# A graph attention layer on one core: a ring of 16 for the gathered rows, loads and stores on other queues in the first stages, a shorter last stage

## The chip, the cores and the metric

The kernel runs on one core of a Trainium2 chip. The metric is the device time of one execution in microseconds (us). The core has a tensor engine (PE, with its weight load shown apart as PEld), a vector engine (DVE), a scalar engine (ACT), a general engine (POOL, GpSimd) and a sync engine (SP) that here only issues transfers. ACT, SP and POOL each have a DMA queue, and an engine that issues a transfer does nothing else in that time.

## The reference

A graph has N = 12500 nodes with 96 features and E = 412500 edges sorted by destination. Keys, queries and values come from the nodes, a factor from each edge; each edge gives 8 heads a weight, and the destination sums weighted values.

```python
Q_h, K_h, V_h = [(x @ W + b).reshape(N, 8, 12) for W, b in ((Wq, bq), (Wk, bk), (Wv, bv))]
E = (edge_attr @ We + be).reshape(-1, 8, 12)
score = K_h[src] * Q_h[dst] / sqrt(12) * E
score = exp(clip(score.sum(-1, keepdims=True), -5.0, 5.0))
wV = segment_sum(V_h[src] * score, dst); Z = segment_sum(score, dst)
out = layernorm(x + wV / (Z + 1e-06))
```

## The kernel before, in words

Every engine runs its own program, written out by hand, and waits on semaphores; no scheduler moves anything.

**First stage** (25 batches of 500 nodes). Per batch: a load of x (`load_x`, two transfers: 112 rows and 13 rows) into a ring of 4 (`x_in`), four transposes on PE, a copy to `xT` (which shares its memory with `accT`) by ACT, four matmuls with the key and value weights, copies to `kv_out` (a ring of 4) by ACT and DVE, and two transfers to `kv_dram`, the table of keys and values. SP issues the loads and the stores alike, in one program (`node_batch`). The matmuls need a row of ones under `xT`, which POOL writes. POOL also loads the edge lists (`dst_nat`, `src_nat`), converts them and stores the destinations in 16 bits. From batch 9 on PE and DVE put in, between batches, 7 blocks of destinations and 7 of sources (`turn`, `destinations`, `sources`: tables `rel` and `src_tab`). When the last is done, DVE makes the least destination of each chunk (`ranges`), POOL stores it and loads it back as the tables `base_tab`, `extra_tab` and `base_all`.

**Query stage** (25 batches). PE makes the queries; ACT and DVE split them into three bf16 parts in `q_out`, a ring of 4 batches (semaphores `q_first`, `q_second`, `q_parts_ready`); SP stores them to `q_dram`. Ahead of the first such store SP issues six transfers of edge features (`load_edges`) and two of destinations. In the middle DVE runs `tables`: it subtracts `base_all` from `rel`.

**Main loop** (806 chunks of 512 edges). POOL gathers the rows of the sources, four indirect transfers (`indirect_dma_start`) per chunk of 128 rows of 768 bytes, into the ring `kv` of RING = 8 chunks; for chunk s it waits until the messages of chunk s-8 are made (`msg_ready`), and, every fourth chunk, until ACT has copied the next four chunks of indices (`copy_sources`, `src_copied`; ACT's step s copies those of chunk s + IDX_AHEAD). ACT makes a one-hot matrix of the destinations, PE turns it into the queries and projects the edge features, DVE multiplies (`kqe`), sums per head, makes the messages, and adds the sums of each chunk into `accT`. SP loads the queries of 8 chunks ahead, ACT the edge features of 15 chunks ahead. At step -1 DVE and ACT each set half of `accT` to zero.

**Last stage** (25 batches). PE transposes `accT`, DVE adds 1e-6 to Z, takes its reciprocal and multiplies, POOL adds x, DVE takes the statistics, ACT the square root and the scaling, SP stores.

Of the kernel before, what the change touches and what calls it, by code (L numbers as in the profile page):

```python
# [5 lines left out]
ALU = mybir.AluOpType  # L6
# [7 lines left out]
P = 128  # L14
HEADS = 8
G = 4
# [14 lines left out]
RING = 8  # L31
HALF = RING // 2
# [5 lines left out]
IDX_AHEAD = 8  # L38
# [3 lines left out]
NOWHERE = -1.0e6  # L42
# [7 lines left out]

def run_steps(engine, step, chunks, lag, round_values=None, lead=0, unroll=RING, ahead=0):

    rounds = (chunks - 1 - ahead) // unroll
    for s in range(-lead, unroll):
        step(s, s % unroll, None)
    with engine.Fori(1, rounds) as i:
# [7 lines left out]
def run_batches(engine, step, batches, lag, shift=0, unroll=4):  # L64

    rounds = (batches - 1 - shift) // unroll
# [9 lines left out]
def gnn_kernel(nc, x, src, dst, edge_attr, Wq, bq, Wk, bk, We, be, Wv, bv, out):  # L79
# [26 lines left out]
    with ExitStack() as ctx:  # L106
# [3 lines left out]
        def sem(name):  # L110
# [14 lines left out]
        kv_mem = sb("kv_mem", [P, RING * G * 2 * D])  # L125
# [5 lines left out]
        src_nat = ea_mem[0:NQ, 0:NJ * CHUNK]  # L131
        dst16 = ea_mem[0:NQ, NJ * CHUNK:NJ * CHUNK * 3 // 2].bitcast(I16)
        q_out = ea_mem[:, NJ * CHUNK * 3 // 2:NJ * CHUNK * 3 // 2 + 2 * BATCH * PARTS * D].bitcast(BF16).rearrange(
            "p (u j k d) -> p u j k d", j=BATCH, k=PARTS, d=D)
        msg_mem = sb("msg_mem", [P, MSG_RING * G * DZ])
        msg = msg_mem[:, :].rearrange("p (c g f) -> p c g f", g=G, f=DZ)
        q_rest = msg_mem[:, 0:2 * BATCH * D].rearrange("p (u j d) -> p u j d", j=BATCH, d=D)
        zero = sb("zero", [P, 1])
# [4 lines left out]
        spare = sb("spare", [P, NJ * CHUNK])  # L143
        dst_nat = spare[0:NQ, 0:NJ * CHUNK]
# [9 lines left out]
        extra_tab = sb("extra_tab", [1, C], I32)  # L154
        most = sb("most", [1, 1], I32)
        base_all = sb("base_all", [P, C], I32)
        minus_id = sb("minus_id", [SEL, C])
        rel = sb("rel", [P, C * G])
        src_tab = sb("src_tab", [P, C * G])
# [16 lines left out]
        x_res = spare[:, 0:4 * BATCH * D].rearrange("p (u j d) -> p u j d", j=BATCH, d=D)  # L176
# [4 lines left out]
        eps = sb("eps", [P, 1])  # L181
        std = sb("std", [P, 2, BATCH])
# [16 lines left out]
        ones_ready = sem("ones_ready")  # L199
        zero_set = sem("zero_set")  # L200
# [46 lines left out]
        kv_in = [sem(f"kv_in{i}") for i in range(RING)]  # L247
# [43 lines left out]
        eps_set = sem("eps_set")  # L291
        rooted = sem("rooted")
# [19 lines left out]
        def landed(engine, sems, c, u, per_load):  # L312

            if isinstance(c, int):
                engine.wait_ge(sems[u], per_load * (c // RING + 1))
# [822 lines left out]
```

## Time and profile before

| | |
|---|---|
| time, median of 3 runs | 4268.54 us (4266.72 to 4269.54) |
| the profiled execution | 4274.5 us, of which the span of its trace is 4272.3 us |
| PE busy | 3085.4 us, 72% of the span |
| DVE busy | 2724.9 us, 64% |
| ACT busy | 1402.3 us, 33% |
| POOL busy | 3164.7 us, 74% |
| bytes moved | 612.49 MB, 143 GB/s over the span |

Busy time leaves out the issue of transfers on ACT and SP; POOL's indirect transfers are counted as busy time of POOL. "Granted clock" is that of the tensor engine, as a share of its full speed of 2.4 GHz.

### The profile page before, as it was taken

To read this page: it belongs to the slowest core of one execution; us is meant where nothing else is said; L and a number is where in the kernel's file an instruction comes from. 1 tells how busy PE (TensorE), PEld (TensorE's weight loads), DVE (VectorE), ACT (ScalarE), POOL (GpSimd) and SP (SyncE) were. 2 spreads that over 40 slices of the span, in tenths; PEclk is the share of its full clock that TensorE was granted. 3 is DMA by queue.
4 is the path that set the end of the run, shared out by engine and by line. 5 is a ranking of instruction groups with operands and counts; after the bars stand their busy time and mean duration, and the time that the engine had idled before them with its cause. 6 is when DMAs were issued, how large, how long until landed. Compare 5 with 4: busy or idle time off the path is not lost.

```text
span 4272.3 us, 62447 instructions
## 1 busy us (share of the span) xinstructions
PE 3085.4 (72%) x16776; PEld 2975.1 (70%) x16777; DVE 2724.9 (64%) x6880; ACT 1402.3 (33%) x3655; POOL 3164.7 (74%) x3356
## 2 busy tenths in 40 slices
PE   6687777777777777777777777777777777777775
PEld 5687766777767677767777767677677766767774
DVE  3676666666666666666666666666666666666667
ACT  2433333333333333333333333333333333333334
POOL 4577777777777777777777777777777777777775
PEclk8555555555555555555555555555555555555555
DMA  7776666666666666666666666666666666666653
GB/s 196 185 154 140 145 140 141 142 143 142 140 144 140 140 143 143 142 139 145 142 138 146 142 140 144 140 142 142 143 142 138 146 140 141 143 142 142 140 129 108
DMA packets 1533277, 612.49 MB, mean 143 GB/s; under 512 B 1392691, under 2 KB 1453694, under 8 KB 1533249
## 3 DMA queue, kind: packets, MB, share of 16 engines
q0 software_dynamic: 156864, 321.70, 30.1%
q10 hardware_dynamic: 1244934, 238.82, 29.4%
q1 hardware_dynamic: 131451, 51.67, 4.9%
q8 instruction: 9, 0.15, 0.0%
q14 instruction: 19, 0.16, 0.0%
HBM read 589.46 MB, written 22.46 MB: 143 GB/s over the span
## 4 chain that ended last, share of the span: by engine, by line
POOL 52%; issue 20%; DMA 12%; DVE 9%; POOLq 1%; DVEq 1%; ACT 0%; ACTq 0%
POOL kv_mem L564 52%; DMA kv_mem<-kv_table,src_idx 12%; DVE kqe L991 2%; DVE kqe L988 2%; DVE msg_mem L1003 2%; DVE oh L1000 1%; DVE raw_score L995 0%; DVE y_stats L1097 0%; DVEq L323 0%; DVE eaT L1011 0%; POOLq L48 0%; ACTq L368 0%; POOLq L562 0%; DVE z_inv L1086 0%; DVE mean_var L1110 0%
## 5 line engine op out<-in xcount | busy, mean ns | idle before, releaser
L564 POOL DMA_INDIRECT kv_mem<-kv_table,src_idx x3224 | 3085.3, 957 | 1012.6 <-issue 928.5
L680 PE MATMUL bank<-w_e,eaT 97*128 97x96 f32 x6448 | 1627.4, 434 | 1076.2 <-DVE eaT L1011 1073.8
L680 PEld LDWEIGHTS bank<-w_e,eaT 97*128 97x128 f32 x6448 | 1440.2, 328 | 1165.7 <-DVE eaT L1011 1159.1
L690 PE MATMUL bank<-oh,msg_mem 128*104 128x32 f32 x6448 | 1258.1, 359 | 7.8 <-DVE msg_mem L1003 7.8
L690 PEld LDWEIGHTS bank<-oh,msg_mem 128*104 128x104 f32 x6448 | 1211.1, 293 | 8.3 <-DVE msg_mem L1003 8.3
L988 DVE TENSOR_TENSOR kqe<-kv_mem,bank 128x384 f32<-128x384 f32 x806 | 445.7, 553 | 1046.0 <-DMA kv_mem<-kv_table,src_idx 1041.9
L797 ACT ACTIVATE msg_mem<-score 128x32 f32<-128x32 f32 x806 | 184.7, 229 | 2711.9 <-DVE score L1017 2464.1
L803 ACT ACTIVATE away<-dst_b,minus_id 96x512 bf16<-96x512 int16 x806 | 568.6, 705 | 0.0
L1011 DVE STREAM_TRANSPOSE eaT<-ea_mem 96x512 f32<-96x512 f32 x806 | 564.8, 701 | 0.0
L806 ACT ACTIVATE ohT<-away 96x512 bf16<-96x512 bf16 x806 | 507.3, 629 | 25.5
L991 DVE TENSOR_TENSOR kqe<-kqe,bank 128x384 f32<-128x384 f32 x806 | 446.1, 553 | 27.8
L995 DVE TENSOR_REDUCE raw_score<-kqe 128x32 f32<-128x384 f32 x806 | 445.5, 553 | 27.8
L1003 DVE TENSOR_TENSOR msg_mem<-kv_mem,bank 128x384 f32<-128x384 f32 x806 | 438.3, 544 | 0.0
L684 PE MATMUL bank<-q_win,ohT 96*128 96x96 bf16 x3224 | 425.2, 283 | 9.5 <-DMA q_win<-q_table 9.5
L684 PEld LDWEIGHTS bank<-q_win,ohT 96*128 96x128 bf16 x3224 | 414.4, 161 | 17.5 <-DMA q_win<-q_table 10.0
L985 DVE TENSOR_TENSOR accT<-bank,accT 104x32 f32 x806 | 154.7, 192 | 331.2 <-DVE score L1017 162.8
L1000 DVE TENSOR_TENSOR oh<-bank,rel 128x128 f32<-128x128 f32 x806 | 226.4, 281 | 6.4 <-ACT bank L799 6.3
L1017 DVE TENSOR_SCALAR score<-raw_score 128x32 f32<-128x32 f32 x806 | 150.2, 186 | 0.0
L799 ACT ACTIVATE bank<-score 128x32 f32<-128x32 f32 x806 | 147.3, 183 | 0.1
L651 PE MATMUL bank<-w_kvq,accT 97*125 97x96 f32 x200 | 36.7, 372 | 23.5 <-DVE msg_mem L949 22.7
L651 PEld LDWEIGHTS bank<-w_kvq,accT 97*125 97x125 f32 x200 | 35.8, 285 | 24.4 <-DVE msg_mem L949 23.4
L587 POOL TENSOR_TENSOR kv_mem<-kv_mem,spare 125x384 f32<-125x384 f32 x25 | 25.0, 1001 | 34.5 <-DVE kv_mem L1091 34.4
(93 smaller groups left out, 516.5 us busy)
## 6 DMA issues: line engine op xcount, KB each, us to landing
ea_mem<-in_edge_attr_dram ACTq DMA_DIRECT2D x591, 256.0 KB
dst_b<-dst_by_chunk ACTq DMA_DIRECT2D x199, 408.0 KB
kv_mem<-kv_table,src_idx POOLq DMA_INDIRECT x3224
q_win<-q_table SPq DMA_DIRECT2D x806, 19.9 KB
kv_table<-kv_mem SPq DMA_DIRECT2D x25, 336.0 KB
q_table<-ea_mem SPq DMA_DIRECT2D x25, 252.0 KB
kv_mem<-in_x_dram SPq DMA_DIRECT2D x25, 168.0 KB
spare<-in_x_dram SPq DMA_DIRECT2D x25, 168.0 KB
```

The lines of the kernel that those rows point to most:

```text
L564: pool.indirect_dma_start(kv[:, slot, g, :], None, kv_dram[:, :], bass.IndirectOffsetOnAxis(ap=src_idx[:, u, g:g + 1], axis=0)).then_inc(k ...
L680: nc.tensor.matmul(e_ps[v][:, g * D:(g + 1) * D], eaT[:, v, g * P:(g + 1) * P], w_e[:, :], start=True, stop=True)
L684: last = nc.tensor.matmul(q_ps[v][:, g * D:(g + 1) * D], ohT[:, u, g * P:(g + 1) * P], q_win[0:SEL, u, :], start=(g == 0), stop=(g == G - ...
L690: last = nc.tensor.matmul(sum_ps[v], msg[:, w, g, :], oh[:, w % DEPTH, g, :], start=(g == 0), stop=(g == G - 1), skip_group_check=True)
L803: nc.scalar.activation(away[:, u % 2, :], dst_b[0:SEL, w, :], ACT.Abs, bias=minus_id[:, bass.ds(t, 1)]).then_inc(away_done, 1)
L806: nc.scalar.activation(ohT[:, w, :], away[:, u % 2, :], ACT.Relu, bias=1.0, scale=-1.0).then_inc(ohT_built, 1)
L988: nc.vector.tensor_tensor(kqe[:, :, :], kv[:, ua, :, 0:D], q_ps[v][:, 0:G * D].rearrange("p (g d) -> p g d", g=G), ALU.mult).then_inc(kq_d ...
L991: nc.vector.tensor_tensor(kqe[:, :, :], kqe[:, :, :], e_ps[v].rearrange("p (g d) -> p g d", g=G), ALU.mult).then_inc(kqe_done, 1)
L995: nc.vector.tensor_reduce(raw_score[:, :], kqe[:, :, :].rearrange("p g (h d) -> p (g h) d", d=HD), AX_X, ALU.add).then_inc(heads_summed, 1)
L1000: nc.vector.tensor_tensor(oh[:, um % DEPTH, :, :], column_ps[um % DEPTH].unsqueeze(1).to_broadcast((P, G, WIN)), rel[:, bass.ds(m * G, G)] ...
L1003: nc.vector.tensor_tensor(msg[:, um % MSG_RING, :, 0:D].rearrange("p g (h d) -> p g h d", d=HD), kv[:, um, :, D:2 * D].rearrange("p g (h d ...
L1011: nc.vector.transpose(eaT[0:D, w % DEPTH, :], ea[:, w, :]).then_inc(ea_turned, 1)
```

## The change

The change has four parts. (1) The rows' ring `kv` has KV_RING = 16 chunks; POOL may run `room` chunks ahead, 16 for the first chunks and one fewer every 6 chunks down to 8; the copies of the indices run 12 chunks ahead, and 16 chunks of indices are copied before the main loop. To make space `rel` and `src_tab` are of 16 bits, and the edge lists and `q_out` lie elsewhere. (2) In the first stage ACT's queue issues the loads of x, SP's only the stores; DVE writes the ones under `xT`, batch by batch; the store of the pad rows and the edge loads come later on SP. ACT's queue stores the queries. (3) POOL loads the three tables back after its first chunk of gathers. (4) 1e-6 is laid into `accT`'s rows of Z at the start (so DVE's half is set in two instructions), the addition in the last stage falls away, and ACT loads the table of the square root once ahead of the last stage.

```diff
-IDX_AHEAD = 8
+IDX_AHEAD = 12
+KV_RING = 16
-        kv_mem = sb("kv_mem", [P, RING * G * 2 * D])
+        kv_mem = sb("kv_mem", [P, KV_RING * G * 2 * D])
-        rel = sb("rel", [P, C * G])
-        src_tab = sb("src_tab", [P, C * G])
+        rel = sb("rel", [P, C * G], I16)
+        src_tab = sb("src_tab", [P, C * G], I16)
...
         @block.sync
-            def node_batch(b, u):
-                if not isinstance(b, int) or 4 <= b < BATCHES:
-                    sp.wait_ge(x_turned, b - 3)
-                    load_x(sp, b, u)
-                if not isinstance(b, int) or b >= 3:
...
+            def store_rows(b, u):
+                sp.wait_ge(kv_evac_act, b + 1)
+                sp.wait_ge(kv_evac_dve, b + 1)
+                for lo, hi in NODE_PARTS:
+                    sp.dma_start(kv_t[lo:hi, bass.ds(b * BATCH, BATCH), :], kv_out[lo:hi, u, :, :]).then_inc(kv_stored[u], 16)
...
-            sp.wait_ge(src_turned, NJ)
             sp.wait_ge(dst16_stored, 32)
-            for g in range(2):
-                load_edges(sp, g * EA_GROUP, g)
             for h in range(2):
                 load_destinations(sp, h * HALF, h)
-            def store_queries(b, u):
...
+            sp.wait_ge(src_made, NJ + 1)
+            load_edges(sp, 0, 0)
+            sp.wait_ge(q_parts_ready, BATCHES // 2)
+            load_edges(sp, EA_GROUP, 1)
...
         @block.gpsimd
-            nc.gpsimd.memset(xT[D:DA, 4 * BATCH * NP:N], 1.0).then_inc(ones_ready, 1)
...
             def step(s, u, _):
-                slot = u % RING
-                at_least(pool, msg_ready, s - RING + 1)
+                slot = u % KV_RING
+                if isinstance(s, int) and s == 1:
+                    load_tables()
+                room = max(KV_RING // 2, KV_RING - max(0, s - KV_RING) // 6) if isinstance(s, int) else KV_RING // 2
+                at_least(pool, msg_ready, s - room + 1)
...
         @block.scalar
             def node_batch(b, u):
...
+                if not isinstance(b, int) or b + 4 < BATCHES:
+                    load_x(act, b + 4, u)
...
-            for s in range(0, IDX_AHEAD, IDX_GROUP):
+            for s in range(0, IDX_RING, IDX_GROUP):
                 copy_sources(s, s)
             def query_batch(b, u):
...
+                if not isinstance(b, int) or b >= 2:
+                    v = (u - 2) % 4
+                    act.wait_ge(q_parts_ready, b - 1)
+                    for lo, hi in NODE_PARTS:
+                        act.dma_start(q_t[lo:hi, bass.ds((b - 2) * BATCH, BATCH), :, :], q_out[lo:hi, v, :, :, :]).then_inc(q_stored[v], 16)
...
+            nc.scalar.activation(table_warm[:, :], eps[:, :], ACT.Sqrt)
...
         @block.vector
             for b in range(1, BATCHES + 1):
+                if b + 3 < BATCHES:
+                    nc.vector.memset(xT[D:DA, (b + 3) * BATCH * NP:(b + 4) * BATCH * NP], 1.0).then_inc(x_ones_set, 1)
...
-                    nc.vector.memset(accT[:, 0:N // 2], 0.0).then_inc(acc_zeroed, 1)
+                    nc.vector.memset(accT[0:D, 0:N // 2], 0.0)
+                    nc.vector.memset(accT[D:P, 0:N // 2], 1e-6).then_inc(acc_zeroed, 1)
...
-                    nc.vector.tensor_scalar(zi, sums[:, :, D:DZ], 1e-6, None, ALU.add).then_inc(z_step, 1)
+                    nc.vector.reciprocal(zi, sums[:, :, D:DZ]).then_inc(z_step, 1)
                 if first:
-                    dve.wait_ge(z_step, 2 * b + 1)
-                    nc.vector.reciprocal(zi, zi).then_inc(z_step, 1)
```

SP's queue between the first and the query stage, before: the last stores of keys and values, the edge features, the destinations, then the first stores of queries (the names are destination <- source and the shape).

```order
L404 DMA kv_table<-kv_mem 112x768 [waits kv_evac_dve,kv_evac_act]
L404 DMA kv_table<-kv_mem 13x768
L368 DMA ea_mem<-in_edge_attr_dram 32x64x32 [waits dst16_stored,src_turned]
L368 DMA ea_mem<-in_edge_attr_dram 32x64x32 x5
L384 DMA dst_b<-dst_by_chunk 102x2048 x2
L437 DMA q_table<-ea_mem 112x1152 [waits q_parts_ready]
L437 DMA q_table<-ea_mem 13x1152
```

The same place now: three edge transfers follow the destinations, three more wait for the middle of the query stage, and no store of queries is on this queue.

```order
L405 DMA kv_table<-kv_mem 112x768 [waits kv_evac_dve,kv_evac_act]
L405 DMA kv_table<-kv_mem 13x768
L413 DMA q_table<-pad_rows 44x288 [waits pad_zeroed]
L390 DMA dst_b<-dst_by_chunk 102x2048 [waits dst16_stored]
L390 DMA dst_b<-dst_by_chunk 102x2048
L374 DMA ea_mem<-in_edge_attr_dram 32x64x32 [waits src_made]
L374 DMA ea_mem<-in_edge_attr_dram 32x64x32 x2
L374 DMA ea_mem<-in_edge_attr_dram 32x64x32 [waits q_parts_ready]
```

POOL from the loads of the tables to chunk 9, before.

```order
L552 DMA base_tab<-chunk_base 1x13x62 [waits range_stored]
L553 DMA extra_tab<-chunk_extra_windows 1x13x62
L554 DMA base_all<-chunk_base 128x806
L564 DMA kv_mem<-kv_table,src_idx 128x192 [waits kv_stored3,src_copied,kv_stored2,kv_stored0,kv_stored1]
L564 DMA kv_mem<-kv_table,src_idx 128x192 x15
L564 DMA kv_mem<-kv_table,src_idx 128x192 [waits src_copied]
L564 DMA kv_mem<-kv_table,src_idx 128x192 x15
L564 DMA kv_mem<-kv_table,src_idx 128x192 [waits msg_ready,src_copied]
L564 DMA kv_mem<-kv_table,src_idx 128x192 x3
```

The same now, up to chunk 16: the first wait for a message stands behind 64 gathers instead of 32, and the tables' loads behind the first four.

```order
L565 DMA kv_mem<-kv_table,src_idx 128x192 [waits dst16_stored,kv_stored3,src_copied,kv_stored2,kv_stored0,kv_stored1]
L565 DMA kv_mem<-kv_table,src_idx 128x192 x3
L546 DMA base_tab<-chunk_base 1x13x62 [waits range_stored]
L547 DMA id_mem<-chunk_extra_windows 1x13x62
L548 DMA base_all<-chunk_base 128x806
L565 DMA kv_mem<-kv_table,src_idx 128x192 x12
L565 DMA kv_mem<-kv_table,src_idx 128x192 [waits src_copied]
...
L565 DMA kv_mem<-kv_table,src_idx 128x192 [waits msg_ready,src_copied]
L565 DMA kv_mem<-kv_table,src_idx 128x192 x3
```

ACT in the first stage now, one batch in the middle: the two loads of x stand between its two copies (before, only the copies were there).

```order
L753 ISA [waits x_turned]
L753 COPY accT<-bank 96x500
L395 ISA
L395 DMA kv_mem<-in_x_dram 112x384
L395 ISA
L395 DMA kv_mem<-in_x_dram 13x384
L760 ISA [waits kv_stored1]
L761 COPY kv_mem<-bank 125x384 [waits kv_done]
```

## Rows read from the trace of the kernel before

**Rows 1.** Page, part 5, main loop: line, engine, count, busy, mean ns, idle before.

```profile
L564 POOL DMA_INDIRECT kv_mem<-kv_table,src_idx x3224 | 3085.3, 957 | 1012.6 <-issue 928.5
...
L1000 DVE TENSOR_TENSOR oh<-bank,rel 128x128 f32<-128x128 f32 x806 | 226.4, 281 | 6.4 <-ACT bank L799 6.3
```

**Rows 2.** Timeline of POOL: start, duration, line, [idle before <- what ended it].

```profile
99.40 1.06 POOL L564 DMA_INDIRECT kv_mem<-kv_table,src_idx  x1 [2.03 <-issue]
...
135.58 4.34 POOL L564 DMA_INDIRECT kv_mem<-kv_table,src_idx  x1 [0.30 <-issue]
...
172.68 0.95 POOL L564 DMA_INDIRECT kv_mem<-kv_table,src_idx  x1 [28.98 <-DVE msg_mem L1003]
...
4194.34 0.95 POOL L564 DMA_INDIRECT kv_mem<-kv_table,src_idx  x1 [0.30 <-issue]
```

**Rows 3.** Waits in 0 to 100 us: total, times, longest.

```profile
PE bank L610 <- DMA kv_mem<-in_x_dram: 24.9, 14, 12.7
```

**Rows 4.** Timeline of SP's queue in the first stage.

```profile
20.57 0.31 SPq L411 DMA_DIRECT2D q_table<-pad_rows  x1
...
83.55 0.86 SPq L404 DMA_DIRECT2D kv_table<-kv_mem  x2
84.62 0.87 SPq L389 DMA_DIRECT2D kv_mem<-in_x_dram  x2
```

**Rows 5.** Windows: length, busy of each engine (count), granted clock, DMA share, GB/s.

```profile
0.00:50.00 50.00, 23.42 (x108) 21.01 (x110) 7.60 (x18) 10.84 (x20) 41.67 (x50) 0.72 0.68 189
50.00:100.00 50.00, 43.27 (x303) 40.14 (x302) 30.15 (x61) 20.00 (x41) 4.25 (x8) 0.97 0.70 200
```

**Rows 6.** Timeline of DVE and ACT in one batch of the first stage.

```profile
82.16 0.64 DVE L891 COPY src_tab<-bank 128x460 f32<-128x460 f32 x1 [0.43 <-PE bank L632]
...
82.59 0.57 ACT L753 COPY accT<-bank 96x500 f32<-96x500 f32 x1 [0.99 <-PE bank L610]
82.71 0.55 DVE L876 COPY kv_mem<-bank 125x384 f32<-125x384 f32 x1
83.18 0.68 DVE L888 TENSOR_REDUCE lohi<-spare 115x1 f32<-115x512 f32 x1
83.30 0.48 ACT L759 COPY kv_mem<-bank 125x384 f32<-125x384 f32 x1
...
93.51 0.56 DVE L876 COPY kv_mem<-bank 125x384 f32<-125x384 f32 x1 [0.74 <-PE bank L625]
```

**Rows 7.** Timeline of POOL: loads of the tables.

```profile
95.79 0.50 POOL L552 DMA_DIRECT2D base_tab<-chunk_base  x1 [4.06 <-DMA chunk_extra_windows<-lohi_end_i]
...
96.77 0.60 POOL L554 DMA_DIRECT2D base_all<-chunk_base  x1
```

**Rows 8.** Timeline of the query stage, ACT, DVE and SP's queue.

```profile
108.19 50.43 SPq L437 DMA_DIRECT2D q_table<-ea_mem  x50
118.95 0.48 ACT L780 CAST ea_mem<-bank 125x384 bf16<-125x384 f32 x1 [19.82 <-DMA q_table<-ea_mem]
119.33 0.52 ACT L784 CAST ea_mem<-msg_mem 125x384 bf16<-125x384 f32 x1
...
135.59 3.50 DVE L921 TENSOR_TENSOR rel<-rel,base_all 128x3224 f32<-128x3224 f32 x1
...
156.10 1.22 DVE L953 TENSOR_TENSOR ea_mem<-msg_mem,ea_mem 125x384 bf16<-125x384 f32 x2
```

**Rows 9.** Timeline of DVE and ACT as the main loop starts.

```profile
160.76 5.27 DVE L1014 MEMSET accT<- 128x6250 f32 x1 [1.26 <-issue]
...
166.95 0.56 DVE L988 TENSOR_TENSOR kqe<-kv_mem,bank 128x384 f32<-128x384 f32 x1 [0.93 <-PE bank L684]
...
182.50 0.19 ACT L768 CAST src_idx<-src_tab 128x16 int32<-128x16 f32 x1
```

**Rows 10.** Timeline of DVE in the last stage, one batch apart.

```profile
4218.23 0.16 DVE L1083 TENSOR_SCALAR z_inv<-bank 125x32 f32<-125x32 f32 x1
...
4220.51 0.16 DVE L1083 TENSOR_SCALAR z_inv<-bank 125x32 f32<-125x32 f32 x1
```

More of the change, by code:

```diff
@@ L41 @@
 BATCH = 4
[L42 removed]
+NOWHERE = -20000
 def at_least(engine, sem, value):
@@ L48, in at_least, with run_steps @@
         engine.wait_ge(sem, value)
-def run_steps(engine, step, chunks, lag, round_values=None, lead=0, unroll=RING, ahead=0):
+def run_steps(engine, step, chunks, lag, round_values=None, lead=0, unroll=RING, ahead=0, first=1):
     rounds = (chunks - 1 - ahead) // unroll
-    for s in range(-lead, unroll):
+    for s in range(-lead, first * unroll):
         step(s, s % unroll, None)
-    with engine.Fori(1, rounds) as i:
+    with engine.Fori(first, rounds) as i:
         values = [None] * unroll if round_values is None else round_values(i)
@@ L61, in run_steps, with run_batches @@
         step(s, s % unroll, None)
-def run_batches(engine, step, batches, lag, shift=0, unroll=4):
-    rounds = (batches - 1 - shift) // unroll
+def run_batches(engine, step, batches, lag, shift=0, unroll=4, ahead=0):
+    rounds = (batches - 1 - shift - ahead) // unroll
     for b in range(unroll + shift):
@@ L246, in gnn_kernel @@
         slots_taken = sem("slots_taken")
-        kv_in = [sem(f"kv_in{i}") for i in range(RING)]
+        kv_in = [sem(f"kv_in{i}") for i in range(KV_RING)]
         pe_step = sem("pe_step")
@@ L566, in step @@
                                             ).then_inc(kv_in[slot], 16)
-            run_steps(pool, step, C, 0, unroll=IDX_RING)
+            run_steps(pool, step, C, 0, unroll=IDX_RING, first=4)
             def gather(c):
@@ L616, in node_batch @@
                         pe.wait_ge(w_kvq_in, 16 * 6)
-                    if isinstance(b, int) and b == 4:
-                        pe.wait_ge(ones_ready, 2)
                     m = b - 1
+                    at_least(pe, x_ones_set, m - 3)
                     pe.wait_ge(x_copied, b)
@@ L807, in step @@
                     if isinstance(s, int) and s == -1:
-                        nc.scalar.copy(accT[:, N // 2:N], zero[:, 0:1].to_broadcast((P, N - N // 2))).then_inc(acc_zeroed, 1)
+                        nc.scalar.copy(accT[:, N // 2:N], acc_first[:, 0:1].to_broadcast((P, N - N // 2))).then_inc(acc_zeroed, 1)
                     if w % HALF == HALF - 1 and (not isinstance(t, int) or t + HALF + 1 < C):
                         load_destinations(act, t + HALF + 1, w // HALF)
-                if u % IDX_GROUP == 0 and (not isinstance(s, int) or s >= 0):
+                if u % IDX_GROUP == 0 and (not isinstance(s, int) or s > 0):
                     copy_sources(s + IDX_AHEAD, (u + IDX_AHEAD) % IDX_RING)
@@ L854, in _ @@
             nc.vector.memset(eps[:, :], EPS_LN).then_inc(eps_set, 1)
+            nc.vector.memset(acc_first[0:D, :], 0.0).then_inc(acc_first_set, 1)
+            nc.vector.memset(acc_first[D:P, :], 1e-6).then_inc(acc_first_set, 1)
             nc.vector.memset(zero[:, :], 0.0).then_inc(zero_set, 1)
```

71 lines of the change are left out of this document (35 added, 36 removed).

## The prediction

> **What bounds the kernel now.** I read the page first, for the main loop. POOL's indirect transfers take 3085.3 us and are followed by idle time put down to "issue" [rows 1]: 957 ns of work and about 0.30 us of gap, 1.26 us per gather and 5.04 us per chunk. Nothing else is as slow, and nearly all that POOL waits for is its own issue. So I went to POOL's timeline for the only times when it does not run at that pace [rows 2]. It starts at 99.40, makes 32 gathers (the ring of 8 chunks is full), stands still for 28.98 us until DVE has made the first messages, starts again at 172.68 and runs to 4195.29 (4194.34 + 0.95). From 172.68 that is 798 chunks in 4022.6 us, 5.041 us each, without one stop. The time of the kernel is therefore: the start of POOL's first gather (99.4), 806 chunks at 5.041 (4063.0), a stop of 28.7 beyond the usual gap, 4.2 us of disturbed gathers, and 77.0 us from the last gather to the end of the span (4272.3). The edit touches the first, third and last of these; the rate stays.
>
> **First stage (POOL's first gather).** That gather waits for the stores of keys and values; the last copy to `kv_out` ends at 94.07 [rows 6] and the gather follows 5.3 us later. What holds the stage is the loads of x: PE waits 24.9 us for them in 14 pieces, the longest of 12.7 us [rows 3], because SP stands until 20.57 at the pad store, behind POOL's memset, with everything queued behind it [rows 4]. Later SP needs 0.86 for a pair of stores and 0.87 for a pair of loads, beside their waits; the pair-to-pair pace there is about 2.2 us at best. Now ACT issues the loads right after its copy of x, four batches ahead, and SP has half its work.
>
> What binds next? DVE's rows for a batch with a turned block are 0.64 + 0.55 + 0.68 [rows 6]; the new memset of 500 columns is estimated from the one of 6250 columns, 5.27 us or, with the unexplained 1.26 us ahead of it, 6.53 [rows 9], so 0.42 to 0.52. Together 2.4 us. ACT has 0.57 + 0.48 and a pair of issues, 0.87 by SP's row: 1.9 us. The transfers: 189 GB/s over 50 us and 200 GB/s over the next 44 [rows 5] are 18.3 MB, and 200 GB/s took a share of 0.70, so 286 GB/s and 64 us if the DMA engines were never idle. At nine tenths of that it is 71 us, against 25 x 2.4 = 60 us plus a start of some 8 us by DVE. The two bounds lie close together; I take the last copy at 72.7, so the first gather at 78.0: **-21.4 us**. Bounds: DMA engines always full, copy at 64.5, gather at 70 (-29); only something like the 12.7 us gap is saved and the rest paces on (-10).
>
> **Tables.** POOL's three loads (95.79 to 97.37, [rows 7]) move behind the first chunk's gathers. They no longer wait 4.06 us for the ranges to be stored, since five microseconds of gathers lie between; but what lay in the shadow of the stores of keys and values now stands between gathers: **+1.6 us**, at most 3.6 if the 2.03 us idle ahead of the first gather [rows 2] comes twice.
>
> **The stop of POOL.** It vanishes if POOL is never out of room or of indices. It needs its first message and the indices of chunks 16 to 19 when it has made 64 gathers: 16 x 5.04 + 1.6 + 4.2 = 86.4 us after its start, at 164.5. Those indices are copied in ACT's step 4, which before came at 182.50, 15.6 us after the first `kqe` at 166.95 [rows 9]. When is the first `kqe` now? I let the query stage start 1.7 us after the last copy, at 74.4. Before, ACT waited 19.82 us in it because SP's edge transfers stood ahead of the stores of queries [rows 8]; these are now on ACT. ACT's batch is 0.48 + 0.52 [rows 8] + a pair of issues of 0.87 = 1.87 us, 47 us for 25. Half the edge transfers still compete; SP's 50 stores took 50.43 us with gathers beside them, or 2.0 per batch. I take 53 us: the last part at 127.5. From there to `kqe` it took 9.6 us (157.32 to 166.95); the second memset on DVE adds up to 6.5: 143.6. Then the indices come at 159.2, 5 us ahead of need. The later groups are looser: POOL needs 20.2 us for four chunks, while DVE's busy time is 3.4 us per chunk (2724.9 / 806) and PE's 3.8 (3085.4 / 806), so both catch up. So the stop goes wholly: **-28.7 us**. The bound on the other side: each microsecond that the query stage takes beyond 58 us comes back one for one.
>
> **What the earlier gathers meet.** Of POOL's first 32 gathers one took 4.34 us instead of 0.96, beside DVE's L921 of 3.50 us [rows 2, 8], and the others lost 0.9 us together (143.70 - 99.40 = 44.3 us, against 40.0 at 1.26 each), beside some 16 of the L953. Before, that was hidden by the stop in part; in my sum it stays in full, and the other nine L953 add **+0.5 us**. L921 reads two tensors from SBUF. The Trainium skill's page "SBUF — State Buffer", section "Who interferes with whom", says that such an instruction contends with a GpSimd instruction that reads SBUF, but also that a probe did not see `tensor_tensor` delay the writing of descriptors. By the second half the disturbance would be nothing and the sum some 4 us lower, 4212; the row of 4.34 us speaks against that.
>
> **Last stage.** One batch takes DVE 2.28 us (4218.23 to 4220.51, [rows 10]), it never waits there, and 0.16 of it is the addition that falls away, with a little of a semaphore: 0.18 x 25, **-4.5 us** (bounds 0, if ACT or POOL takes over the pace, and 5). The early load of the square root's table costs ACT nothing, it stands idle then. The rows of Z starting at 1e-6 cost nothing but the second memset, already counted.
>
> **Sum.** -21.4 - 28.7 + 1.6 + 0.5 - 4.5 = -52.5 us. The profiled execution, 4274.5, becomes 4222.0; it stands 6.0 above the median of the runs shown, 4268.5, so the forecast for a median is **4216 us**.
>
> **Rivals.**
> A. *The first stage doesn't speed up much*, because transfers are slower when more of them are in flight: gather at 89, so -10 instead of -21: 4227. For it: the share is 0.70 already [rows 5]. Against: PE's waits are of the loads' lateness, not their length.
> B. *The new wait for indices or messages.* If the query stage takes 65 us instead of 53, for ACT now issues inside it and waits for `q_stored` with a ring of 4, POOL stops for about 7 us at chunk 16: 4223; at 75 us, 4233. For it: by the same start of 1.7 us the old stage took 157.3 - 95.8 = 61.5 us, though 19.8 of them were the block by edges.
> C. *DVE's memsets hold POOL.* POOL was standing while L1014 ran, so no row shows it. If they held it as L921 did, two of 6.5 us would add 13: 4229. Against: L1000, with one input from SBUF, leaves the gather's mean at 957 ns [rows 1]. The page named above agrees with this: an instruction with at most one SBUF input outside the two-port modes does not contend; by it the 13 us are nothing.
> D. *Slower than before: a gather gets longer in the main loop.* The only instruction of the loop whose operand changes type is L1000, which reads `rel`, now in 16 bits; it takes 281 ns per chunk [rows 1]. If it held POOL for all of that, 806 x 0.281 = 226 us would be lost: 4442. It decides from 52.5 us / 806 = 65 ns per chunk, 16 ns per gather. Against: it has one input from PSUM before and after, and POOL's gap does not feel it now.
> E. *Both gains are larger*: the gather starts at 70, and the disturbances shrink: 4205.
>
> **How the numbers follow.** Forecast with its small terms (4208 to 4224) 0.56; A 0.14; B 0.12; C 0.06; D 0.04; E 0.08. The range from 4201 to 4238 leaves out D, the worst of B and the extremes of A with C, and less than 2 in 10. A difference of 0.2% (8.5 us) is about what can be told from no change. All but D, and A, B and C together (0.02), are beyond it: faster 0.94, same 0.02, slower 0.04.
>
> **What would show it.** In the changed kernel's trace: the first gather at 74 to 82 and not near 89; PE's wait for x under 8 us; no idle of POOL above 3 us before the last gather, in particular none at chunk 16, 20 or 24; a spacing of gathers of 1.26 us; one gather of about 4.3 us beside the subtraction; none stretched beside the memsets; the last gather at about 4148; a batch of the last stage in 2.1 us. The prediction is wrong if POOL stops at chunk 16, if its first gather comes after 88, or if the mean of a gather is not 957 ns.

## The result, and the profile after

The changed kernel takes 4206.73 us (median of 4 runs, 4204.96 to 4207.62); the kernel before beside it took 4268.74 us. The ratio is 0.9855, with a 95% interval from 0.9838 to 0.9872: 62 us faster, 10 us more than forecast, and inside the forecast range of 4201 to 4238. The profiled execution of the changed kernel took 4206.3 us, its span 4204.4 us.

POOL's timeline is the one to read first, as before. Start, duration, line, [idle before <- what ended it].

```profile
70.71 1.05 POOL L565 DMA_INDIRECT kv_mem<-kv_table,src_idx  x1 [5.81 <-DMA kv_table<-kv_mem]
...
74.62 0.96 POOL L565 DMA_INDIRECT kv_mem<-kv_table,src_idx  x1 [0.30 <-issue]
75.58 0.56 POOL L546 DMA_DIRECT2D base_tab<-chunk_base  x1
...
76.67 0.59 POOL L548 DMA_DIRECT2D base_all<-chunk_base  x1
...
101.14 4.50 POOL L565 DMA_INDIRECT kv_mem<-kv_table,src_idx  x1 [0.30 <-issue]
...
136.76 0.95 POOL L565 DMA_INDIRECT kv_mem<-kv_table,src_idx  x1 [0.30 <-issue]
...
158.20 0.95 POOL L565 DMA_INDIRECT kv_mem<-kv_table,src_idx  x1 [0.39 <-issue]
...
4130.10 0.95 POOL L565 DMA_INDIRECT kv_mem<-kv_table,src_idx  x1 [0.31 <-issue]
```

The first gather starts at 70.71 instead of 99.40 [rows 2], the three table loads stand behind the fourth gather, the 65th gather (chunk 16) starts at 158.20 with 0.39 us of idle time ahead of it, and nothing stops POOL until its last gather ends at 4131.05. The stop of 28.98 us has no counterpart.

The first stage, in the waits of 0 to 100 us (total, times, longest), the windows (busy time of PE, PEld, DVE, ACT and POOL, granted clock, DMA share, GB/s) and SP's queue:

```profile
PE bank L611 <- DMA kv_mem<-in_x_dram: 6.0, 6, 4.0
```

```profile
0.00:50.00 50.00, 40.68 (x249) 37.61 (x251) 31.49 (x66) 19.21 (x37) 32.75 (x49) 0.97 0.91 293
...
20.00:25.00 5.00, 4.30 (x28) 3.71 (x27) 2.46 (x6) 2.38 (x6) 4.78 (x5) 1.00 1.03 389
...
50.00:60.00 10.00, 9.97 (x75) 9.57 (x73) 9.23 (x18) 5.25 (x10) 0.00 (x0) 1.00 0.68 206
```

```profile
9.74 57.12 SPq L405 DMA_DIRECT2D kv_table<-kv_mem  x50
66.91 1.26 SPq L413 DMA_DIRECT2D q_table<-pad_rows  x1
```

PE's waits for x are 6.0 us instead of 24.9 [rows 3], the stores begin at 9.74, and 293 GB/s moved in the first 50 us instead of 189 [rows 5], at times 389. Near the end of the stage the transfers are not what it waits for: from 50 to 60 us their share is 0.68, and PE is busy for 9.97 of the 10 us. The clock granted to PE in the first 50 us is 0.97 instead of 0.72 [rows 5]; before, PE did nothing from 15 to 20 us, and the clock was 0.50, its lower level, from 20 to 30.

The start of the main loop, on DVE and ACT:

```profile
129.67 5.27 DVE L1028 MEMSET accT<- 96x6250 f32 x1 [1.26 <-issue]
136.28 5.27 DVE L1029 MEMSET accT<- 32x6250 f32 x1 [1.34 <-issue]
141.58 0.55 DVE L1002 TENSOR_TENSOR kqe<-kv_mem,bank 128x384 f32<-128x384 f32 x1
...
145.93 0.55 DVE L1017 TENSOR_TENSOR msg_mem<-kv_mem,bank 128x384 f32<-128x384 f32 x1
...
157.22 0.19 ACT L770 CAST src_idx<-src_tab 128x16 int32<-128x16 int16 x1
```

The page, part 5, and DVE's timeline in the last stage, one batch apart:

```profile
L565 POOL DMA_INDIRECT kv_mem<-kv_table,src_idx x3224 | 3076.2, 954 | 988.2 <-issue 937.6
```

```profile
4188.17 0.33 DVE L1098 RECIPROCAL z_inv<-bank 125x32 f32<-125x32 f32 x1
...
4190.22 0.33 DVE L1098 RECIPROCAL z_inv<-bank 125x32 f32<-125x32 f32 x1
```

A batch takes 2.05 us, against 2.28 [rows 10]. A gather is 954 ns instead of 957 [rows 1]; from the 65th gather to the last their distance is 1.2573 us, in the profile of before 1.2602. So the 67.9 us between the two spans are:

| term | us |
|---|---|
| first gather, 99.40 to 70.71 | -28.7 |
| the stop | -28.7 |
| distance of gathers, 3223 x 0.0029 | -9.4 |
| table loads between gathers (distance of the fourth and fifth is 2.94) | +1.7 |
| stretched gathers: 5.3 us in all, 4.5 before | +0.9 |
| from the last gather's end to the end of the span, 77.0 to 73.35 | -3.7 |

Two of these were not in the forecast at this size: the first, and the third, which was not in it at all.

### The profile page after: what moved, and what is told of

It reads as the page before. It is cut to its first block, busy times and chain, and to the rows that moved or that the text cites. A ratio compares the mean times of both kernels' runs of the same rounds, so it can differ in the third digit from the quotient of the medians.

```text
span 4204.4 us, 62289 instructions
## 1 busy us (share of the span) xinstructions
PE 3076.6 (73%) x16776; PEld 2970.3 (71%) x16777; DVE 2718.5 (65%) x6879; ACT 1402.2 (33%) x3656; POOL 3146.7 (75%) x3355
## 4 chain that ended last, share of the span: by engine, by line
POOL 54%; issue 21%; DMA 12%; DVE 9%; DVEq 1%; PE 1%; POOLq 1%; SPq 1%; ACT 0%; ACTq 0%
POOL kv_mem L565 54%; DMA kv_mem<-kv_table,src_idx 10%; DVE kqe L1005 2%; DVE kqe L1002 2%; DVE msg_mem L1017 2%; DMA q_table<-msg_mem 1%; DVEq L329 1%; DVE oh L1014 1%; DVE eaT L1025 1%; PE bank L625 1%; DVE raw_score L1009 0%; DVE y_stats L1109 0%; SPq L374 0%; POOLq L49 0%; DMA q_win<-q_table 0%
## 5 line engine op out<-in xcount | busy, mean ns | idle before, releaser
L810 ACT ACTIVATE away<-dst_b,id_mem 96x512 bf16<-96x512 int16 x806 | 568.7, 706 | 1.7 <-issue 1.7
L684 PEld LDWEIGHTS bank<-q_win,ohT 96*128 96x128 bf16 x3224 | 414.4, 161 | 19.8 <-DMA q_win<-q_table 12.3
L1014 DVE TENSOR_TENSOR oh<-bank,rel 128x128 f32<-128x128 f32 x806 | 226.2, 281 | 5.9 <-ACT bank L806 5.9
L1032 DVE TENSOR_SCALAR score<-raw_score 128x32 f32<-128x32 f32 x806 | 137.5, 171 | 0.0
L588 POOL TENSOR_TENSOR kv_mem<-kv_mem,x_res 125x384 f32<-125x384 f32 x25 | 25.0, 1001 | 28.7 <-DVE kv_mem L1103 28.7
```

Of the source, the lines that this page charges most:

```text
L684: last = nc.tensor.matmul(q_ps[v][:, g * D:(g + 1) * D], ohT[:, u, g * P:(g + 1) * P], q_win[0:SEL, u, :], start=(g == 0), stop=(g == G - ...
L810: nc.scalar.activation(away[:, u % 2, :], dst_b[0:SEL, w, :], ACT.Abs, bias=minus_id[:, bass.ds(t, 1)]).then_inc(away_done, 1)
L1014: nc.vector.tensor_tensor(oh[:, um % DEPTH, :, :], column_ps[um % DEPTH].unsqueeze(1).to_broadcast((P, G, WIN)), rel[:, bass.ds(m * G, G)] ...
```

## The experiments

The theory: POOL's chain sets the time, so a microsecond at the first gather, in a stop, or behind the last gather is a microsecond of the kernel. The loads of x on a queue of their own bring the early start; the lead of 16 chunks takes the stop away. Rivals: the early start comes from the pad store alone; the stop would have gone with the shorter query stage; the 3 ns per gather belong to the longer ring. The ones that DVE writes, the tables of 16 bits and the higher clock were not tried by themselves.

**Both kernels once more, on one chip** (`r_before`, `r_after`).

> The kernel before, once more, on the chip of the three kernels that follow. In its first profile the gathers of the main loop come every 1.2603 us, in that of the changed kernel every 1.2573 us. Theory 1 (the 3 ns belong to the change): 1.260 here again. Theory 2 (they belong to the execution or the chip): 1.257 to 1.260 here, and the same in the changed kernel of this call. Time 4268 us; first gather at 99.4 us, one stop of 29 us.

> The changed kernel, once more. Theory 1 (the change brings 3 ns per gather, 9.7 us in all): spacing 1.257, time 62 us less than before. Theory 2 (it brings the start and the stop alone, 28.7 + 28.7 + 3.7 - 2 = 59 us): spacing equal to that of the kernel before in this call. First gather at 70.7 us, no stop above 3 us.

Measured: before 4267.81 us (4265.69 to 4270.46, the 13 runs beside these kernels; `r_before` itself 4267.93), changed 4205.04 (4204.51 to 4210.98), ratio 0.9853 [0.9837, 0.987]. In both profiled executions the distance of the gathers was 1.2586 us, and so it was in `e_lead8`; in `e_sp_loads`, on the same chip, it was 1.2573, as in the last four profiles below, from another one. It hardly moves within an execution (1.2582 to 1.2590 over any 512 gathers of these two). So the 3 ns are not the change's: theory 2. The value 1.2602 was seen once, in the first profile of the kernel before; that it could come with the changed kernel is not shown.

The kernel before did not do all that was expected of it: its first gather came at 97.68 and not 99.4, and its stop was longer than 29 us:

```profile
175.44 0.95 POOL L564 DMA_INDIRECT kv_mem<-kv_table,src_idx  x1 [36.54 <-DVE msg_mem L1003]
```

Here DVE's L921 ran at 139.42, inside the stop, so no gather was stretched by it. The first product came at 169.72 (166.95 in the first profile). The spans of this pair, at the same distance, differ by 60.8 us: 28.2 at the first gather (97.68, 69.45), 3.6 behind the last, 29.0 between. In these 29.0 the stop counts 36.2, beyond the usual gap; the changed kernel gives back 3.9 more in stretched gathers, 1.7 for the tables and 1.65 at chunk 16, which comes next.

POOL, in the profiled execution of the changed kernel:

```profile
69.45 1.05 POOL L565 DMA_INDIRECT kv_mem<-kv_table,src_idx  x1 [5.81 <-DMA kv_table<-kv_mem]
...
156.09 0.95 POOL L565 DMA_INDIRECT kv_mem<-kv_table,src_idx  x1 [0.30 <-issue]
158.99 0.95 POOL L565 DMA_INDIRECT kv_mem<-kv_table,src_idx  x1 [1.95 <-issue]
```

and ACT:

```profile
144.24 7.21 ACTq L374 DMA_DIRECT2D ea_mem<-in_edge_attr_dram  x3
...
158.00 0.19 ACT L770 CAST src_idx<-src_tab 128x16 int32<-128x16 int16 x1
```

Chunk 16 waited 1.65 us for the copy of its indices, which stands in ACT's program behind three edge transfers. The gather starts 0.80 us after the copy's end, and so it does in the first profile (157.22 + 0.19, 158.20): there too the copy let the gather go, 0.1 us late. There is no slack at that place.

**The lead alone undone** (`e_lead8`).

```diff
-                room = max(KV_RING // 2, KV_RING - max(0, s - KV_RING) // 6) if isinstance(s, int) else KV_RING // 2
+                room = KV_RING // 2
```

> The changed kernel with POOL allowed only 8 chunks ahead from the start; the ring's memory of 16 chunks stays. Theory 1 (the stop is gone because of the lead): 32 gathers end at 117.6 us in the changed kernel's trace and the first messages are made at 146.5 us, so POOL stands for some 29 us at chunk 8 and the time is 29 us longer, 4235 us. Rival (the query stage now ends so early that the lead is hardly needed): a stop under 10 us and 4217 us or less. If the spacing of the gathers is 1.257 us here, the longer lead is not what changed it.

Measured: 4233.28 us (4232.58 to 4236.02), 28.2 more than the changed kernel on the same chip, ratio to before 0.9919 [0.9903, 0.9936]. POOL, at chunk 8:

```profile
114.17 0.95 POOL L565 DMA_INDIRECT kv_mem<-kv_table,src_idx  x1 [0.30 <-issue]
143.49 0.95 POOL L565 DMA_INDIRECT kv_mem<-kv_table,src_idx  x1 [28.36 <-DVE msg_mem L1017]
```

The stop is back in full, ended by the first message, and costs what it lasts. The distance of the gathers was 1.2586 us here as well, with the short lead. The lead is needed, and the shorter query stage would not have done it: the whole front moved forward, gathers and messages alike.

**The loads of x back on SP's queue** (`e_sp_loads`). The pad store stays behind the stores, the ones stay with DVE.

```diff
-            def store_rows(b, u):
...
+            def node_batch(b, u):
+                if not isinstance(b, int) or 4 <= b < BATCHES:
+                    sp.wait_ge(x_turned, b - 3)
+                    load_x(sp, b, u)
+                if not isinstance(b, int) or b >= 3:
+                    m, um = b - 3, (u - 3) % 4
...
-                if not isinstance(b, int) or b + 4 < BATCHES:
-                    load_x(act, b + 4, u)
```

> The changed kernel, but SP's queue issues the loads of x again, beside the stores; the pad store stays behind them all, and DVE still writes the ones. Theory 1 (the early first gather comes mostly from SP no longer standing at the pad store until 20.6 us; the share of two queues is small): first gather at 74 to 78 us, PE waits for x some 10 us, time 3 to 8 us more. Theory 2 (SP's serial loads and stores pace the stage at 2.2 us a batch and more): first gather at 85 to 90 us, time 15 to 20 us more. Each microsecond at the first gather should come back as one at the end.

Measured: 4224.85 us (4221.14 to 4227.79), 19.8 more than the changed kernel; its first gather, PE's waits for x and the waits of SP's queue:

```profile
89.94 1.35 POOL L570 DMA_INDIRECT kv_mem<-kv_table,src_idx  x1 [7.69 <-DMA kv_table<-kv_mem]
```

```profile
PE bank L616 <- DMA kv_mem<-in_x_dram: 23.2, 17, 5.4
SPq L408 <- DVE kv_mem L891: 25.7, 20, 5.2
```

Theory 2: 20.5 us later, and 19.8 in the time. With the long pause at the pad store gone, PE still waits 23 us for x, now in 17 short pieces. The second line is SP's queue: it waits 25.7 us for DVE's copies, ahead of stores, and the next batch's loads stand behind. The profile shows no wait of SP for a load's slot, so it is the loads that are held, not the stores. With two queues they are not.

**The pad store ahead of the stores** (`e_pad_first`), and **the tables loaded ahead of the gathers** (`e_tables_first`).

```diff
-            run_batches(sp, store_rows, BATCHES, 0)
             sp.wait_ge(pad_zeroed, 1)
             sp.dma_start(q_dram[N * PARTS:N_PAD * PARTS, :].rearrange("(n k) d -> n (k d)", k=PARTS), pad_rows[:, :]).then_inc(pad_stored, 16)
+            run_batches(sp, store_rows, BATCHES, 0)
```

```diff
+            load_tables()
             wait_all(pool, kv_stored)
...
-                if isinstance(s, int) and s == 1:
-                    load_tables()
```

> The changed kernel with one thing moved back: SP issues the pad store, which waits for POOL's memset, ahead of its stores of keys and values (ACT still issues the loads of x). Theory 1 (with the loads on ACT's queue a late SP costs little, since a ring of 4 batches and a lighter queue catch up): SP stands until about 20 us, the first store should have gone at 9.7 us; first gather 0 to 3 us later than 70 us. Theory 2 (the stage paces on the full DMA engines, so what isn't moved in the first 20 us is moved later): first gather 5 to 10 us later, and the time by as much.

> The changed kernel with POOL's three table loads ahead of its first gather again. Theory 1 (they are hidden behind the landing of the last stores of keys and values, 5.8 us of idle time ahead of the first gather, so moving them behind the first chunk costs 1.7 us): here POOL waits for the ranges to land (4 us in the kernel before), its loads end about at the time of the first gather, the gap of 2.94 us behind the fourth gather is 1.26, and the time is 0 to 2 us less. Theory 2 (the wait for the ranges, 62.1 us + 4, and three loads of 0.5 us reach past 70 us): first gather 1 to 3 us later, time the same or 1 us more.

These two, and `e_zadd` and `e_q_sp` below, ran on another chip, on which the kernel before takes 5470.15 us (5463.96 to 5484.54): in the main loop there POOL makes 16 gathers and stands some 6 us for a message, again and again, so their times (5449.38 and 5432.00) are not used. Up to the first gather its four profiles are like the others: 79.29 here with the pad store first, and 69.63, 68.25 and 68.58 without. ACT, in `e_pad_first`:

```profile
24.89 0.48 ACT L761 COPY kv_mem<-bank 125x384 f32<-125x384 f32 x1 [9.18 <-DMA kv_table<-kv_mem]
```

SP issued the pad store at 20.49 and the first row store at 20.91; by 15.7 us the ring of 4 in `kv_out` was full, and ACT stood 9.2 us. The stage ended 10 us later, the size that theory 2 gave. What is late is not caught up: from the end of ACT's fifth copy of keys and values to the end of its last it takes 48.2 us here (25.4 to 73.6) and 47.5 in the changed kernel (17.7 to 65.2). But theory 2 put this down to full DMA engines, and while from 30 to 50 us their share is still some 0.9, near the end of the stage the one that is full is PE:

```profile
60.00:70.00 10.00, 9.97 (x76) 9.60 (x74) 9.43 (x18) 4.78 (x9) 0.00 (x0) 1.00 0.70 213
```

The pad store costs some 10 us when the queues are two, the shared queue some 20 when the pad store is late; together the change brought 28.

In `e_tables_first` POOL's idle time was filled:

```profile
67.09 0.50 POOL L546 DMA_DIRECT2D base_tab<-chunk_base  x1 [3.95 <-DMA chunk_extra_windows<-lohi_end_i]
...
68.07 0.59 POOL L548 DMA_DIRECT2D base_all<-chunk_base  x1
69.63 1.05 POOL L564 DMA_INDIRECT kv_mem<-kv_table,src_idx  x1 [0.96 <-DMA kv_table<-kv_mem]
```

It still waits 0.96 us for the stores of keys and values, so the loads fitted ahead, and from the fourth gather to the fifth it is 1.26 us: moving the tables behind the first chunk costs the changed kernel 1.7 us and brings nothing, as theory 1 had it.

**Two more on that chip** (`e_zadd`, `e_q_sp`) have the edits of the next two experiments.

> The changed kernel with its fourth part undone but for the early load of the square root's table: DVE sets its half of the accumulator with one memset, and adds 1e-6 in the last stage. Theory 1 (DVE paces the last stage): a batch of the last stage takes 2.28 us instead of 2.05, and the time from the last gather to the end of the span is 77 us instead of 73.4; at the start the first product comes 6.6 us earlier, at 134 to 135 us, and nothing follows from that but the 0 to 1.7 us of the stop at chunk 16. Time +2 to +4 us. Rival (the last stage is not paced by DVE's addition but by a wait, and the second memset costs as much as it brings): time the same within 1 us.

> The changed kernel with the queries stored by SP's queue again, behind all six edge transfers. Theory 1 (POOL has no slack at chunk 16, so each microsecond of the query stage beyond that of the changed kernel is a stop): ACT stands for its ring of 4 some 20 us instead of 9, the first product comes 3 to 10 us later than 141 us, POOL stops at chunk 16 by the same amount, and the time is that much longer. Rival (the edges take the same 36 us of the transfers wherever the stores are issued, so the stage lasts as long): first product within 2 us, time the same within 2 us.

At 5451.07 us (5430.24 to 5468.45) and 5458.31 us (5438.88 to 5468.61) they decide nothing: POOL stands 47 us at chunk 16 in the one and 64 in the other, and 65 in `e_tables_first`, which stores the queries as the changed kernel does. The next two have these edits on a chip where the kernel before takes 4266.98 us.

**The last stage as before** (`e_zadd_2`): one memset by DVE, and the addition of 1e-6 in each batch. ACT's half of `accT` starts at zero too.

```diff
-            nc.vector.memset(acc_first[D:P, :], 1e-6).then_inc(acc_first_set, 1)
+            nc.vector.memset(acc_first[D:P, :], 0.0).then_inc(acc_first_set, 1)
...
-                    nc.vector.memset(accT[0:D, 0:N // 2], 0.0)
-                    nc.vector.memset(accT[D:P, 0:N // 2], 1e-6).then_inc(acc_zeroed, 1)
+                    nc.vector.memset(accT[:, 0:N // 2], 0.0).then_inc(acc_zeroed, 1)
...
-                    nc.vector.reciprocal(zi, sums[:, :, D:DZ]).then_inc(z_step, 1)
+                    nc.vector.tensor_scalar(zi, sums[:, :, D:DZ], 1e-6, None, ALU.add).then_inc(z_step, 1)
...
+                    nc.vector.reciprocal(zi, zi).then_inc(z_step, 1)
```

> The changed kernel with one memset of DVE for its half of the accumulator and the addition of 1e-6 in the last stage, as e_zadd; that ran on a chip where the main loop has another bound. Theory 1: a batch of the last stage takes 2.28 us instead of 2.05, 77 us from the last gather to the end instead of 73.4; the first product comes 6.6 us earlier, at 134 to 135 us, and brings nothing beyond the stop of 0 to 2 us at chunk 16. Time +2 to +4 us. Rival: the same within 1 us.

Measured: 4212.57 us (4209.93 to 4213.68), against 4207.49 (4205.73 to 4209.78) for the changed kernel beside it (`r_after_2`): +5.1. DVE, as the main loop starts and in the last stage:

```profile
127.77 5.27 DVE L1028 MEMSET accT<- 128x6250 f32 x1 [1.26 <-issue]
136.37 0.56 DVE L1002 TENSOR_TENSOR kqe<-kv_mem,bank 128x384 f32<-128x384 f32 x1 [3.33 <-PE bank L684]
...
4186.43 0.16 DVE L1097 TENSOR_SCALAR z_inv<-bank 125x32 f32<-125x32 f32 x1
...
4188.71 0.16 DVE L1097 TENSOR_SCALAR z_inv<-bank 125x32 f32<-125x32 f32 x1
```

The period is 2.28 us again, theory 1, and from the last gather to the end it takes 78.9 us, more than the 77.0 of before. Two things differ from what was expected. The second memset is only 3.7 us on the path to the first product (140.02 in `r_after_2`, 136.37 here), for without it DVE waits 3.33 us for PE. And the addition is worth 5.1 us, not 3.6: in the 24 distances of DVE's multiplications the changed kernel takes 48.8 us, this one 53.8, the kernel before 54.4. The rest hides at the very end, see below.

**The queries stored by SP again** (`e_q_sp_2`), behind all six edge transfers. These are two changes in one: the queue of the stores, and the place of three edge transfers.

```diff
             load_edges(sp, 0, 0)
-            sp.wait_ge(q_parts_ready, BATCHES // 2)
             load_edges(sp, EA_GROUP, 1)
...
+            run_batches(sp, store_queries, BATCHES, 0)
...
-                if not isinstance(b, int) or b >= 2:
-                    v = (u - 2) % 4
-                    act.wait_ge(q_parts_ready, b - 1)
-                    for lo, hi in NODE_PARTS:
...
-            run_batches(act, query_batch, BATCHES, 2, 1)
+            run_batches(act, query_batch, BATCHES, 1, 1)
```

> The changed kernel with the queries stored by SP behind all six edge transfers, as e_q_sp, in which ACT stood 22.9 us for its ring of 4 and 5.0 us once more, against 8.2 to 9.9 us in the kernels that store by ACT. Theory 1 (no slack at chunk 16): the query stage ends some 15 us later, the first product comes at about 155 us, POOL stops at chunk 16 by about 14 us, time +14 us. Rival (the edges take their 36 us of the transfers either way and the stage catches up): first product at 141 to 146 us, time +0 to +5 us.

Measured: 4216.32 us (4213.92 to 4218.92), +8.8. ACT in the query stage, and POOL at chunk 16:

```profile
92.26 0.48 ACT L788 CAST msg_mem<-bank 125x384 bf16<-125x384 f32 x1 [22.51 <-DMA q_table<-msg_mem]
```

```profile
156.03 0.95 POOL L571 DMA_INDIRECT kv_mem<-kv_table,src_idx  x1 [0.30 <-issue]
165.73 0.95 POOL L571 DMA_INDIRECT kv_mem<-kv_table,src_idx  x1 [8.75 <-issue]
```

The mechanism of theory 1, in the 3 to 10 us of the first expectation and below the 14 of the second: the block is 14 us longer than in `r_after_2` (22.5, 8.4), the stage catches up 5 of it, as the rival said in part (first product at 148.74, 8.7 later), and POOL's stop of 8.4 us beyond the usual gap is nearly the difference of the times.

**A better version** (`e_best`), beside `r_after_2` on one chip.

```diff
+            sp.wait_ge(range_stored, 64)
+            sp.dma_start(base_tab[:, :], base_dram.rearrange("(a c) -> a c", a=1)).then_inc(tabs_in, 16)
...
-                if isinstance(s, int) and s == 1:
-                    load_tables()
...
+                if isinstance(s, int) and s in (0, 4):
+                    for k in ((0, 1) if s == 0 else (2,)):
+                        for c in range(k * IDX_GROUP, (k + 1) * IDX_GROUP):
+                            act.wait_ge(kv_in[c], 16 * G)
+                        copy_sources(IDX_RING + k * IDX_GROUP, k * IDX_GROUP)
...
+                if BATCHES // 2 <= b < BATCHES // 2 + PIECES:
+                    subtract_bases(b - BATCHES // 2)
```

> The changed kernel once more, on the chip of the three kernels that follow, to compare them with. Theory 1 (POOL has no slack at chunk 16, and its pace is of the execution and not of the kernel): first gather at 69 to 71 us, no stop or one of up to 2 us at chunk 16, gathers every 1.257 to 1.260 us, 4205 us. If the kernel before takes some 5470 us here again, then the chip is as the one of the last four runs, and only what comes before the gathers can be read.

> The changed kernel with three more edits. (a) SP loads the three tables, POOL's gathers run on without a gap: 1.7 us less. (b) DVE subtracts the bases in 8 pieces of a hundred chunks, one per batch of queries, instead of one instruction of 3.50 us: theory 1 (the long instruction holds one gather for its whole length, short ones of 0.45 us cost a gather 0.3 at most) 1 to 3.4 us less; theory 2 (what counts is the time that DVE reads two tensors of SBUF, however cut) no gain. (c) ACT copies the indices of chunks 16 to 23 at its step 0, those of chunks 24 to 27 at step 4: theory 1 (the index copy, not the message, is what chunk 16 waits for) no stop at chunk 16, though the gathers come earlier by (a) and (b); if the message of chunk 0 is what it waits for, a stop stays. Sum by theory 1: 4 to 6 us less than the changed kernel, 4200 us.

Measured: 4202.56 us (4201.0 to 4203.89), ratio to before 0.9849 [0.9833, 0.9866]; `r_after_2` 4207.49, 0.9861 [0.9844, 0.9877]. The intervals overlap, the runs on the one chip do not: 4.9 us. Of them the traces place 4.3 between the first gather and the end of the last (4060.0 us, 4055.8). The first gather itself was 2.3 us earlier in `e_best`, which none of its edits does: it lies between 68.3 and 71.4 in all profiles with the changed first stage. POOL beside the pieces of the subtraction, and at chunk 16:

```profile
100.84 1.39 POOL L562 DMA_INDIRECT kv_mem<-kv_table,src_idx  x1 [0.30 <-issue]
...
103.94 1.61 POOL L562 DMA_INDIRECT kv_mem<-kv_table,src_idx  x1 [0.31 <-issue]
...
151.93 0.95 POOL L562 DMA_INDIRECT kv_mem<-kv_table,src_idx  x1 [0.31 <-issue]
```

1.7 us are the tables. The long gather (5.12 us to the next one in `r_after_2`) is gone; the four most stretched ones of `e_best` lose 1.5 us together, against 4.4 for the three of `r_after_2`, and over all the first 64 it is 2.4 against 5.0: 2.6 us, theory 1. The pieces took 0.57 us each, not 0.45. The indices of chunks 16 to 23 were there at 136.7 us, 15 before their use. `r_after_2` had no stop (indices at 156.4, chunk 16 at 158.50), but that doesn't make (c) idle. At the place in ACT's program from which chunk 16's indices came before, `e_best` makes its next copy:

```profile
155.85 0.19 ACT L767 CAST src_idx<-src_tab 128x16 int32<-128x16 int16 x1
```

With the 0.8 us seen above a gather could follow it at 156.8, and chunk 16 now starts at 151.93. By this estimate (a) and (b) without (c) would have been lost in a stop of some 5 us. (c) was not run alone, nor left out alone.

## Why the prediction was right, step by step

The steps hold: POOL's chain sets the end, the edit touches its start, its stop and its tail, and none of the rivals that cost time decided it. But the time, 4206.7 us, lies below the 4208 to 4224 that had a chance of 0.56, next to rival E (gather at 70, 4205 us, chance 0.08): its earlier start came true, while the disturbances did not shrink.

- **First stage.** Mechanism right, size off: -21.4 forecast, -28.7 and -28.2 measured. The mis-sized step is the bound by the transfers, from which the last copy was put at 72.7 us; it ended at 65.99. The capacity was scaled from a share of 0.70 at 200 GB/s to 286 GB/s at a full share; the changed kernel moved 389 GB/s at a share of 1.03. And the list of what binds next left out PE, which is busy 9.97 of 10 us near the end of the stage (the window from 50 us) at 206 GB/s; nor does the forecast have a term for PE's clock, 0.72 before and 0.97 now. What the clock is worth was not measured. ACT had more room than the forecast's 1.9 us per batch: a copy of 0.57 us starts at 14.06 and its pair of issues, 0.87 long, at 14.07, so, other than said of the engines at the start, ACT issues a transfer while the copy ahead of it still runs. The bound by DVE, 60 + 8 us, was near. Rival A is false; that the shared queue held the stage is shown by `e_sp_loads`.
- **Tables.** +1.6 forecast, +1.7 measured.
- **The stop.** -28.7 forecast and measured in the first pair, and shown to be the lead's by `e_lead8`. The size was read from the very profile that it is compared with; in `r_before` the stop was 36.2 us. The 5 us of slack given for it did not exist. With the earlier start POOL wanted the indices 6.4 us earlier than forecast (158.1, not 164.5), but they came only 1.8 earlier (157.4, not 159.2), because the query stage took 59 us, from 67.31 to 126.24, and not 53. Rival B was half true: `e_q_sp_2` shows that a longer query stage comes back nearly one for one.
- **Stretched gathers.** +0.5 forecast, +0.9 measured in the first pair, +3.9 in the second, where L921 had fallen into the stop. The row of 4.34 us was the right guide: the same operation in 16 bits took 3.50 us and made a gather last 4.50. The Trainium skill, page "SBUF — State Buffer", section "Who interferes with whom", says that an instruction with two inputs in SBUF contends with GpSimd's reads, and infers from a probe that writing descriptors is not held by it. `r_after_2` and `e_best` side by side (4.82 us in one piece, at most 1.61 beside pieces of 0.57) agree with the first sentence; a gather's row doesn't tell reading its indices from writing descriptors, so they don't decide the second.
- **Memsets.** Rival C is false: beside both the gathers lasted 0.95 to 0.96 us (the row at 136.76). The Trainium skill's rule in the same section, that an instruction with at most one input in SBUF doesn't contend, agrees.
- **Rival D** is false: L1014 reads the table in 16 bits, takes 281 ns, and a gather is not longer.
- **Last stage.** -4.5 forecast, -3.7 measured: the addition brought 5.1; `e_zadd_2` is another 0.6 shorter than before in the 24 distances, of which 0.3 stand at the third (2.59 to 2.25 us), where the table was loaded before, and 0.3 at the eleventh, unexplained; 0.2 more fell ahead of the first; and 2.3 were lost again at the end of the span.
- **The rate.** "The rate stays" was right of the kernel. The 9.4 us of the profiled pair come from their executions. A mean of a gather other than 957 ns was named as a sign of being wrong; it was 954 ns in the changed kernel, and 954 ns in `r_before` too, so that sign was narrower than what two executions of one kernel show. Without the 9.4 the terms of the pair make 58.5 us, and the medians differ by 62.0. The 3.5 between are not placed, since only profiled executions show their distance; the profiled one of `r_before`, at 1.2586 us, was the slowest of its eight.

With the first gather at 70.7 the forecast's sum would have been -59.8 us, 4209 us: the start is most of the error of 9.

## What to carry to other kernels

When one engine's chain runs without a gap, count only its start, its stops and its tail; here each microsecond of a stop or a late start came back as one in the time. A queue that issues both loads and stores holds the loads behind the stores' waits: 20 us here, beyond the pause that could be seen. When you ask what binds a stage next, go through every engine: here PE was left out. Before a lead is called sufficient, look for the small copy that feeds it: here the ring was long enough and the indices arrived with no time to spare, so anything that lets the gathers come earlier needs that copy earlier too.

## What the runs showed that was not expected

Where POOL sets the pace, the distance of the gathers had one of three values for a whole execution: 1.2573 or 1.2574 us in six profiles, 1.2586 in three, 1.2602 in one. A step is 1.3 or 1.6 ns, 4 to 5 us of the time; the kernel before and the changed one both showed 1.2586. With the stop of 1.65 us such a step would explain why the profiled execution of `r_after` took 4210.98 us and the three others 4204.5 to 4205.6; that is not shown.

In every profile of a changed kernel the span goes on longer behind the last byte. The last windows of `r_before` and of `r_after_2`, in which nothing is busy and no byte moves (columns as above):

```profile
4269.00:4270.00 1.00, 0.00 (x0) 0.00 (x0) 0.00 (x0) 0.00 (x0) 0.00 (x0) 0.50 0.00 0
```

```profile
4201.80:4204.80 3.00, 0.00 (x0) 0.00 (x0) 0.00 (x0) 0.00 (x0) 0.00 (x0) 0.50 0.00 0
```

That is 1.0 us in `r_before`, 3.0 in `r_after_2`: from ACT's last instruction to the end of the span 2.8 and 5.1 us. `e_zadd_2` has it too, so it isn't the addition. The cause is open; nothing was tried on it.

One of the chips was different. On it engines stood idle between two instructions of one group with no wait to show for it. The page, part 5, of `e_tables_first`:

```profile
L679 PE MATMUL bank<-w_e,eaT 97*128 97x96 f32 x6448 | 1728.4, 419 | 1776.8 <-issue 1524.7
```

It begins only when the gathers run. The four variants of the changed kernel were 12 to 38 us faster than before there, and POOL, which waits for messages every 16 gathers, was no longer the bound. What starves the engines on that chip is open.
